# Second biases of an FFN and of eight experts taken off TensorE, zeros added into open sums, and the places of a tanh stage dealt out anew

## The chip, the cores and the metric

The kernel runs on one core of a Trainium2 chip. The metric is the device time of one execution in microseconds (us), and the figure compared is the median over runs.

## The reference, cut to what matters

The input is x, 4 batches of 1024 tokens, 256 wide, all in float32. The first layer is an additive cross-attention to 77 context rows of each batch; the second is a mixture of 8 experts beside a shared FFN.

```python
txt_proj = einsum('btd,de->bte', textual_features, Ws)
feat_proj = einsum('bfd,de->bfe', layernorm(x), W)
h = tanh(txt_proj[:, None, :, :] + feat_proj[:, :, None, :] + b)     # 1024 x 77 x 256 per batch
rho = einsum('bftd,d->bft', h, w[:, 0]) + (1 - qm)[:, None, :] * NEG
att = softmax(rho);  txt_h = einsum('bft,btd->bfd', att, textual_features)
x = x + tanh(txt_h @ Wcw.T + bcw) * layernorm(x) + tanh(txt_h @ Wcb.T + bcb)
...
y = layernorm(x)
probs = softmax(y @ gate)                                            # 4096 tokens, 8 experts
scores, token_idx = top_k(probs per expert, k=512)
out_tok = gelu(y[token_idx] @ W1 + b1) @ W2 + b2                      # 256 -> 1024 -> 256
routed = zeros.at[token_idx].add(out_tok * scores)
shared = gelu(y @ Ws1 + bs1) @ Ws2 + bs2
x = x + routed + shared
```

The two biases b2 and bs2 that are added after the second matrix product are the "second biases" of the title.

## The kernel before, in words

The kernel is one program with one list of steps, made by `work_order`. Every engine walks the whole list and runs the steps that are its own, in the list's order; semaphores carry the waits between engines. So an engine that waits at one step holds up all its later ones.

**The tanh stage** (0 to 602 us). Tokens are cut into 8 units of 512 (v = 0 to 7, two in a batch; `va` = 6 and `vb` = 7 are the last two). The 1024 x 77 x 256 tanh values of a batch are dealt into blocks of 128 x 4096, 157 in all (0 to 156). A block goes through three steps: `add` on VectorE (L1434: z = feat + one column of txt_bias, 8 adds of 128x512 where the block belongs to one unit, 4 of 128x1024 where it belongs to both units of a batch), `tanh` on ScalarE in place (L1042; a few "direct" pieces, L1038, have ScalarE do the add itself and VectorE none), and `rho` on TensorE (L828), which multiplies by w and adds into a bank of the unit that stays open until the unit's last block. There are 4 buffers z, so the adds of block n+4 need rho(n) to be over; from block 90 on rho goes two blocks at a time (`TOGETHER`). `SPLITS` tells which blocks are of both units, and so where a unit ends: unit 6 ends with block 144 and unit 7 with block 156.

Between the blocks stands everything else, at places given by the tables `PRE` (x's layer norm, its turn, the projection, of the next units), `TAIL` (what follows when a unit's sums are complete) and `FFN` (the shared FFN of units 0 to 5). What has place n comes behind add(n+2), tanh(n+1) and rho(n) in the list. The tail of a unit is, in order: rho_out and rho_turn; `att_shift` (VectorE, L1493 to L1497), `att_exp` (ScalarE, L1049), `weigh` (VectorE), `gate_in` (L1528, L1530), `gates` (ScalarE, L1053), `y_scale` (POOL, the nine small instructions from L1244 to L1257), `logits_shift` (VectorE, L1613 to L1617, reads POOL's y_ry), `y_norm` (POOL, L1173 and L1176), the turning of y on TensorE (L754), and four `whole` steps (POOL, L1300). These last complete the residual in x_ring.

The shared FFN runs m by m over 8 slices of 128 of H: `up` (TensorE L870, 6 matmuls), `gelu` (ScalarE, L1096), `down` (TensorE, L885, four 128x256 matmuls into two open banks). Before slice 0 the bias bs2 is put in by four matmuls (L881): a row of zeros and ones, `b2_row`, times `b2_s`, in which VectorE has split b2 and bs2 into two parts (`split_b2`, once, early). Then `down_end` (VectorE L1649) adds the banks to x_ring, and the result is stored.

**The router** (602 to 666 us). Unit 7's tail, the softmax of all logits and ten rounds of a threshold search, then ranks and lists. The FFN of units 6 and 7 is cut into 97 pieces which TensorE runs between the rounds ("filler").

**The experts** (666 to 862 us). For each expert `e_up` (L954), gelu, a split in two parts (`e_hi` ScalarE L1142, `e_lo` VectorE L1796), `e_down` and `e_sum` (L977). Before slice 0 four matmuls (L971) put in the bias b2; for the last expert there is one (L987) before each of its four tiles (L992). `e_out` (ScalarE L1150) scales a 128x256 tile by the tokens' scores, and POOL scatters it, adding, into the output (L1355). W1 and W2 of the next expert are loaded by SP and split meanwhile.

## Time and profile before

| | |
|---|---|
| median of 3 runs | 871.35 us (870.77 to 871.72) |
| the profiled execution, its device time | 871.33 us |
| its span, first to last instruction | 869.5 us |
| busy: TensorE, ScalarE, VectorE, POOL | 791.8, 752.7, 714.6, 272.1 us |
| mean granted TensorE clock | 0.983 of full speed |

Read it by stages: each engine's share over the whole span is a mean over three stages that have different limits. The time outside the span is 871.33 - 869.5 = 1.8 us.

### The profile page before, as it was taken

The numbers are of one execution on the slowest core, as the hardware profiler recorded it, in microseconds if no ns is written. First come the engines' busy times: TensorE is split into PE (matmuls) and PEld (weight loads), VectorE is DVE, ScalarE is ACT, GpSimd is POOL, SyncE is SP. The second block draws the span as 40 slices with busy tenths as digits, with TensorE's granted clock in tenths as the row PEclk, the third lists the DMA queues.
The fourth block names the chain that finished last, engine by engine and source line by source line (L and its number), as shares of the span: only waits on it lengthen the run. The fifth ranks groups of instructions, "written<-read, shape, count | busy, mean of one in ns | idle before, by whom it ended". The sixth has DMA issues, their size and how long they took to land.

```text
span 869.5 us, 13896 instructions
## 1 busy us (share of the span) xinstructions
PE 791.8 (91%) x5385; PEld 475.6 (55%) x5385; DVE 714.6 (82%) x1408; ACT 752.7 (87%) x556; POOL 272.1 (31%) x388
## 2 busy tenths in 40 slices
PE   7776677659999999999999999999999999999996
PEld 6321122214444344444444554564777999999986
DVE  4789999997979999999799989998887776666540
ACT  3999999999999999999999999988854676667672
POOL 3200430053505004784001360014504144555424
PEclk9798999999999999999999999999999999999999
DMA  7100000000001000200000010002203356554513
GB/s 258 33 1 1 1 1 1 1 25 25 2 1 49 1 1 1 98 1 2 25 1 1 25 49 1 25 2 76 95 25 106 126 133 147 146 144 100 135 21 41
DMA packets 32405, 41.81 MB, mean 48 GB/s; under 512 B 2365, under 2 KB 29011, under 8 KB 32339
## 3 DMA queue, kind: packets, MB, share of 16 engines
q1 hardware_dynamic: 26083, 32.49, 11.5%
q0 software_dynamic: 6144, 8.39, 5.7%
q8 instruction: 43, 0.70, 0.3%
q14 instruction: 23, 0.19, 0.1%
q10 hardware_dynamic: 112, 0.04, 0.0%
HBM read 28.33 MB, written 12.58 MB: 47 GB/s over the span
## 4 chain that ended last, share of the span: by engine, by line
PE 42%; ACT 40%; DVE 8%; issue 7%; POOL 2%; POOLq 0%; DVEq 0%; ACTq 0%
ACT z L1042 37%; PE bank L954 10%; PE bank L977 9%; PE bank L828 6%; PE bank L885 5%; DVE z L1434 5%; PE bank L870 4%; ACT u L1096 2%; PE bank L754 1%; PE bank L803 1%; PE bank L764 1%; PE bank L992 1%; POOL xn L1176 1%; PE bank L928 1%; PE bank L971 0%
## 5 line engine op out<-in xcount | busy, mean ns | idle before, releaser
L1042 ACT ACTIVATE z<-z 128x4096 f32<-128x4096 f32 (+3 forms) x157 | 536.1, 3481 | 5.9 <-DVE z L1434 5.9
L1434 DVE TENSOR_SCALAR z<-feat,txt_bias 128x1024 f32<-128x1024 f32 (+1 forms) x742 | 431.9, 655 | 18.9 <-PE bank L828 18.3
L828 PE MATMUL bank<-z,window 128*32 128x512 f32 x2464 | 298.4, 612 | 47.6 <-ACT z L1042 47.4
L828 PEld LDWEIGHTS bank<-z,window 128*32 128x32 f32 x2464 | 69.3, 111 | 230.8 <-issue 141.5
L885 PE MATMUL bank<-ws_sb,u 128*128 128x256 f32 x512 | 126.3, 388 | 0.7 <-ACT u L1096 0.6
L885 PEld LDWEIGHTS bank<-ws_sb,u 128*128 128x128 f32 x512 | 92.4, 190 | 35.2 <-issue 20.6
L870 PE MATMUL bank<-tr,ws_s 128*128 128x512 f32 x384 | 107.3, 417 | 2.3 <-ACT u L1096 1.6
L954 PE MATMUL bank<-xg_s,w_s 128*128 128x512 f32 x384 | 99.1, 396 | 0.2 <-DVE xg_s L1790 0.2
L1796 DVE TENSOR_TENSOR hid_s<-hid,hid_s 128x512 fp32r<-128x512 f32 x60 | 41.5, 692 | 59.2 <-ACT hid_s L1142 59.2
L977 PEld LDWEIGHTS bank<-w_s,hid_s 128*128 128x128 f32 x672 | 86.3, 188 | 3.9
L1244 POOL TENSOR_TENSOR scale<-wb,x_ry 128x4 f32<-128x4 f32 x7 | 3.8, 544 | 270.3 <-ACT wb L1053 270.3
L977 PE MATMUL bank<-w_s,hid_s 128*128 128x256 f32 x672 | 88.1, 280 | 0.0
L1132 ACT ACTIVATE hid<-bank,vec 128x512 f32<-128x512 f32 x64 | 44.1, 690 | 49.0 <-PE bank L954 48.9
L870 PEld LDWEIGHTS bank<-tr,ws_s 128*128 128x128 f32 x384 | 70.5, 188 | 29.2 <-issue 11.4
L954 PEld LDWEIGHTS bank<-xg_s,w_s 128*128 128x128 f32 x384 | 68.0, 188 | 12.1 <-DVE xg_s L1790 0.7
L1343 POOL DMA_INDIRECT xg<-xn_dram,idx x32 | 38.4, 1199 | 112.6 <-DVE idx L1779 105.3
L1355 POOL DMA_INDIRECT out_dram<-y,idx x32 | 57.5, 1798 | 30.8 <-ACT y L1150 22.9
L1096 ACT ACTIVATE u<-bank,vec 128x512 f32<-128x512 f32 x64 | 44.4, 704 | 10.7 <-PE bank L870 10.7
L1165 POOL TENSOR_SCALAR x_ve<-x_mv 128x4 f32<-128x4 f32 x7 | 4.3, 613 | 126.3 <-DVE x_less L1380 126.3
L1810 DVE TENSOR_TENSOR w_s<-w_raw,w_s 128x1024 fp32r<-128x1024 f32 (+1 forms) x36 | 39.2, 1103 | 1.3 <-ACT w_s L1117 1.3
L1142 ACT ACTIVATE hid_s<-hid 128x512 fp32r<-128x512 f32 x60 | 38.0, 633 | 1.9
L1176 POOL TENSOR_SCALAR xn<-x_ring,y_ry,offset 128x256 f32<-128x256 f32 x32 | 34.0, 1072 | 0.9
(263 smaller groups left out, 720.7 us busy)
## 6 DMA issues: line engine op xcount, KB each, us to landing
w_raw<-in_L_ffn_W_dram SPq DMA_DIRECT2D x16, 1024.0 KB, 5.6
x_ring<-in_x_dram SPq DMA_DIRECT2D x8, 512.0 KB, 7.9
xn_dram<-xn SPq DMA_DIRECT2D x8, 512.0 KB, 2.9
out_dram<-x_ring SPq DMA_DIRECT2D x8, 512.0 KB, 2.9
u<-in_L_ffn_Ws_dram SPq DMA_DIRECT2D x1, 1024.0 KB, 11.8
ws_sb<-in_L_ffn_Ws_dram SPq DMA_DIRECT2D x1, 1024.0 KB, 14.5
xg<-xn_dram,idx POOLq DMA_INDIRECT x32, 4.5
out_dram<-y,idx POOLq DMA_INDIRECT x32, 4.1
```

Source lines behind the costliest of these rows:

```text
L828: ins = e.matmul(sums[v][32 * g:32 * g + 32, :], window[:, c, 31 - at_row:63 - at_row], z[:, n % ZB, at_piece:at_piece + TOK], start=(v, g ...
L870: ins = e.matmul(dst[:], ws1_s[:, i, c, m * P:(m + 1) * P], tr[:, v % 2, j, c, :], start=n == 0, stop=n == passes - 1)
L885: ins = e.matmul(banks[DOWN[j // 2]][:, j % 2 * D:(j % 2 + 1) * D], u[:, m % UR, j * P:(j + 1) * P], ws2_sb[:, m, :], start=False, stop=m ...
L954: ins = e.matmul(dst[:], w1_s[k][:, i, c, m * P:(m + 1) * P], xg_s[:, k, j, c, :], start=c == 0 and n == 0, stop=c == C - 1 and n == 2)
L977: ins = e.matmul(part, parts[:, i, a * P:(a + 1) * P], w2_s[k][:, j, m, :], start=False, stop=(m == M - 1 and term == 2), skip_group_check ...
L1042: e.activation(part, part, ACT.Tanh).then_inc(signal(*step), 1)
L1096: e.activation(u[:, m % UR], banks[up_bank(v, m)][:], ACT.Gelu_apprx_tanh, bias=vec[:, col["bs1"] + m:col["bs1"] + m + 1]).then_inc(signal ...
L1132: e.activation(hid[:, m % HC, :], banks[UP[m % 2]][:], ACT.Gelu_apprx_tanh, bias=vec[:, cb:cb + 1]).then_inc(signal(*step), 1)
L1176: ins = e.tensor_scalar(dst[:, j, :], src[:, j, :], factor[:, j:j + 1], offset[:, j:j + 1], ALU.mult, ALU.add)
L1355: e.indirect_dma_start(out_rows, where, y[:, ex % 2, a, :], None, compute_op=ALU.add).then_inc(scattered, 16)
L1434: ins = e.tensor_scalar(z[:, n % ZB, i * width:(i + 1) * width], feat_of(units, c), bias_of(units, t, c), None, ALU.add)
L1796: e.tensor_tensor(parts[:, 1, :], hid[:, m % HC, :], parts[:, 0, :].bitcast(F32), ALU.subtract).then_inc(signal(*step), 1)
```

## The change

Seven things change together.

- The second biases leave TensorE. All 64 bias matmuls go: 32 L881, 28 L971 and 4 L987, and with them `split_b2`, one memset and four small DMAs.
- bs2 comes as `bs2_rep`, one row copied to all partitions, and a new POOL step `biased` adds it to x_ring behind the `whole` steps of each unit: four tensor_tensor 128x256, 32 in all. `down_end` now waits for it.
- b2 of all experts comes as `b2_rep` by a broadcast DMA of 1 MB (`load_b2`) behind the first expert's weights, into buffers that are dead by then. A new POOL step `bias_rows` multiplies it by the scores, four tensor_scalar 128x256 per expert at slice 3. `e_out` moves from ScalarE to VectorE: one instruction with bank, score and bias row.
- `stir`: 89 bf16 matmuls of zeros, 128x512, are added to the open sum: two behind rho of blocks 0 to 2 and 8 to 46, and one in the middle of a unit's logits where a sum is open. Three more matmuls on ident stand behind unit 0's logits.
- In the last batch 10 rows are shared by both units where there were 8: four blocks of one unit become blocks of both, unit 6 ends with block 146 and unit 7's own blocks are the last 10 rather than 12.
- Direct pieces in the first blocks are 28 where they were 24, and 1 later where there were 4.
- The tables PRE, TAIL and FFN, the number of filler pieces at each point of the router, and the place of unit 6's `down_end` are dealt out anew. The filler is 97 pieces in both.

```diff
-SPLITS = ((8, 20), (0, 20), (0, 20), (0, 8))
-FIRST_DIRECT = (6, 3, 0, 2, 2, 4, 0, 7)
+SPLITS = ((8, 20), (0, 20), (0, 20), (0, 10))
+FIRST_DIRECT = (7, 7, 1, 3, 1, 4, 0, 5)
 AHEAD = 3
-DIRECT = (8, 9, 126, 129)
+DIRECT = (12,)
...
-    (0, 0, 2, 2, 2, 2, 4, 4, 5, 10, 7, 7, 11, 11, 11),
+    (1, 1, 2, 1, 2, 2, 3, 4, 1, 5, 3, 7, 7, 8, 6),
...
-    (128, 130, 132, 133, 136, 136, 139, 142),
-    (143, 144, 145, 146, 147, 148, 149, 152),
+    (128, 129, 132, 133, 134, 137, 138, 140),
+    (143, 144, 145, 146, 148, 149, 149, 150),
...
-TOGETHER, TOGETHER_FROM = 2, 90
-BUSY = (20, 3, 5)
+TOGETHER, TOGETHER_FROM = 2, 92
+BUSY = (20, 3, 5, 3)
+STIRS = {n: 2 for n in (0, 1, 2, *range(8, 47))}
...
-END_PLACES = (3, 4)
-ENDS_BEHIND = 8
+END_PLACES = (10, 2)
+ENDS_BEHIND = 6
...
-FFN_PLACES = (-1, 1, 2)
+FFN_PLACES = (-1, 0, 2)
...
-                *[[("y_turned", v, c)] for c in range(C)], [("whole", v, j) for j in range(J)]]
+                *[[("y_turned", v, c)] for c in range(C)], [*(("whole", v, j) for j in range(J)), ("biased", v)]]
...
-              ("load_w1", 0), ("load_w2", 0), *end[2], ("att_exp", vb), ("early_probs",)]
+              ("load_w1", 0), ("load_w2", 0), ("load_b2",), *end[2], ("att_exp", vb), ("early_probs",)]
...
+        if m == 3:
+            steps.append(("bias_rows", ex))
...
-            for first in (0, B2_LOW):
-                e.dma_start(b2_raw[first:first + E, :], b2).then_inc(loaded["b2"], 16)
-                e.dma_start(b2_raw[first + E:first + E + 1, :], bs2.unsqueeze(0)).then_inc(loaded["b2"], 16)
+            e.dma_start(bs2_rep[:], bs2.partition_broadcast(P)).then_inc(loaded["bs2"], 16)
...
+                elif kind == "load_b2":
+                    e.wait_ge(*done("rho_turn", vb))
+                    e.dma_start(b2_rep[:], b2.rearrange("e d -> (e d)").partition_broadcast(P).rearrange("p (e d) -> p e d", e=E)
+                                ).then_inc(loaded["b2"], 16)
...
+            def stir(times):
+
+                if not stirred:
+                    e.wait_ge(consts, MASK_CLEAR)
+                    stirred.append(True)
+                held = [v for v in sums if all((v, g) in begun for g in range(G)) and any(left[v, g] for g in range(G))]
+                for _ in range(times if held else 0):
+                    e.matmul(sums[held[-1]][:], spare[:, 0:1].bitcast(BF16)[:, 0:1].broadcast_to([P, P]), ones_h[:], start=False,
+                             stop=False, skip_group_check=True)
...
+                    stir(STIRS.get(n, 0))
...
+                        if j == J // 2:
+                            stir(1)
...
-                        e.wait_ge(*done("split_b2"))
                     if m == 0:
-                        for j in range(first, end):
-                            dst = take(DOWN[j // 2]) if j % 2 == 0 else banks[DOWN[j // 2]]
-                            e.matmul(dst[:, j % 2 * D:(j % 2 + 1) * D], b2_row[:, E:E + 1].broadcast_to([B2_ROWS, P]), b2_s[:],
-                                     start=j % 2 == 0, stop=False, skip_group_check=True)
+                        for j in range(first + first % 2, end, 2):
+                            take(DOWN[j // 2])
                     e.wait_ge(*done("gelu", v, m))
                     for j in range(first, end):
                         ins = e.matmul(banks[DOWN[j // 2]][:, j % 2 * D:(j % 2 + 1) * D], u[:, m % UR, j * P:(j + 1) * P],
-                                       ws2_sb[:, m, :], start=False, stop=m == M - 1, skip_group_check=True)
+                                       ws2_sb[:, m, :], start=m == 0 and j % 2 == 0, stop=m == M - 1, skip_group_check=True)
...
-                        for a in range(A):
-                            e.matmul(sums_of[a // 2][:, a % 2 * D:(a % 2 + 1) * D], b2_row[:, ex:ex + 1].broadcast_to([B2_ROWS, P]), b2_s[:],
-                                     start=a % 2 == 0, stop=False, skip_group_check=True)
...
-                elif kind == "e_out":
-                    ex, a = args
-                    bank, left = (SUM[ex % 2][a // 2], a % 2 * D) if ex < E - 1 else (LAST_SUM[a], 0)
-                    e.wait_ge(*(done("e_sum", ex, a // 2) if ex < E - 1 else done("e_tile", a)))
-                    e.wait_ge(*done("scored", ex))
-                    if ex > 1:
-                        e.wait_ge(scattered, 16 * A * (ex - 1))
-                    e.activation(y[:, ex % 2, a, :], banks[bank][:, left:left + D], ACT.Identity,
-                                 scale=score[:, ex % NL, a:a + 1]).then_inc(signal(*step), 1)
...
+                elif kind == "biased":
+                    v, = args
+                    e.wait_ge(loaded["bs2"], 16)
+                    for j in range(J):
+                        row_of = x_ring[:, v % XB, j, :]
+                        e.wait_ge(*done("whole", v, j))
+                        ins = e.tensor_tensor(row_of, row_of, bs2_rep[:], ALU.add)
+                    ins.then_inc(signal(*step), 1)
...
+                elif kind == "bias_rows":
+
+                    ex, = args
+                    e.wait_ge(loaded["b2"], 16)
+                    e.wait_ge(*done("scored", ex))
+                    if ex > 1:
+                        e.wait_ge(*done("e_out", ex - 2, A - 1))
+                    for a in range(A):
+                        ins = e.tensor_scalar(bias_rows[:, ex % 2, a, :], b2_rep[:, ex, :], score[:, ex % NL, a:a + 1], None, ALU.mult)
                     ins.then_inc(signal(*step), 1)
...
-                    e.wait_ge(*done("whole", v, J - 1))
+                    e.wait_ge(*done("biased", v))
...
+                elif kind == "e_out":
+                    ex, a = args
+                    bank, left = (SUM[ex % 2][a // 2], a % 2 * D) if ex < E - 1 else (LAST_SUM[a], 0)
+                    e.wait_ge(*done("bias_rows", ex))
+                    e.wait_ge(*(done("e_sum", ex, a // 2) if ex < E - 1 else done("e_tile", a)))
+                    e.wait_ge(*done("scored", ex))
+                    if ex > 1:
+                        e.wait_ge(scattered, 16 * A * (ex - 1))
+                    e.scalar_tensor_tensor(out=y[:, ex % 2, a, :], in0=banks[bank][:, left:left + D],
+                                           scalar=score[:, ex % NL, a:a + 1], in1=bias_rows[:, ex % 2, a, :], op0=ALU.mult,
+                                           op1=ALU.add).then_inc(signal(*step), 1)
...
-                elif kind == "split_b2":
-                    low = slice(B2_LOW, 2 * B2_LOW)
-                    e.wait_ge(loaded["b2"], 64)
-                    e.tensor_tensor(b2_row[:], ident[0:B2_ROWS, 0:E + 1], ident[0:B2_ROWS, B2_LOW:B2_LOW + E + 1], ALU.add)
-                    link(e.tensor_copy(b2_s[:], b2_raw))
-                    e.wait_ge(vector_link, linked)
-                    e.tensor_tensor(b2_s[low, :], b2_raw[low, :], b2_s[low, :].bitcast(F32),
                                     ALU.subtract).then_inc(signal(*step), 1)
```

The rows below are each engine's instructions in program order. First TensorE at the first expert, before (`xg` are the gathered tokens, L954 is e_up, L971 the bias, L977 e_down):

```order
L754 MATMUL bank<-ident,xg 128x128 x8
L954 MATMUL bank<-xg_s,w_s_126 128x512 x18
L971 MATMUL bank<-b_s,b_row 128x256 x4
L977 MATMUL bank<-w_s_127,hid_s 128x256 x12
L954 MATMUL bank<-xg_s,w_s_126 128x512 x6
```

and after, where L772 is the turn of xg, L972 is e_up and L990 is e_down:

```order
L772 MATMUL bank<-ident,xg 128x128 x8
L972 MATMUL bank<-xg_s,w_s_125 128x512 x18
L990 MATMUL bank<-w_s_126,hid_s 128x256 x12
L972 MATMUL bank<-xg_s,w_s_125 128x512 x6
L990 MATMUL bank<-w_s_126,hid_s 128x256 x12
```

The bias rows are gone and nothing stands in their place on TensorE.

Next the tail of unit 6, which falls on the last dozen blocks of the tanh stage. VectorE before, at `att_shift` (L1434 are the adds, eight to a block, and two at the end of unit 6 or 7; L1486 is rho_out, L1649 down_end, L1493 to L1497 att_shift):

```order
L1486 COPY rho_sb<-bank 128x512
L1649 TENSOR_TENSOR x_ring<-bank,x_ring 128x512 x2
L1434 TENSOR_SCALAR z<-feat,txt_bias 128x512 x16
L1493 TENSOR_REDUCE bank<-bank 128x4
L1495 TENSOR_REDUCE sm<-bank 128x4
L1497 TENSOR_TENSOR att<-bank,sm 128x320
```

and after, where L1455 are the adds, L1507 is rho_out and L1514 and L1516 begin att_shift:

```order
L1455 TENSOR_SCALAR z<-feat,txt_bias 128x512 x34
L1507 COPY rho_sb<-bank 128x512
L1455 TENSOR_SCALAR z<-feat,txt_bias 128x512 x8
L1514 TENSOR_REDUCE bank<-bank 128x4
L1516 TENSOR_REDUCE sm<-bank 128x4
L1518 TENSOR_TENSOR att<-bank,sm 128x320
```

The adds of four blocks now stand ahead of rho_out, and those of one more between rho_out and att_shift. Before, two blocks' adds stood there. VectorE again, from the last step of `weigh` to `logits_shift` (L1613 to L1617) of unit 6, before:

```order
L1521 TENSOR_REDUCE wb<-att_tmp 128x8
L1434 TENSOR_SCALAR z<-feat,txt_bias 128x512 x16
L1528 TENSOR_TENSOR wb<-wb,sm 128x8
L1530 TENSOR_TENSOR wb<-wb,bc 128x8
L1434 TENSOR_SCALAR z<-feat,txt_bias 128x512 x34
L1613 TENSOR_TENSOR lg<-lg,y_ry 128x32
L1615 TENSOR_REDUCE sm<-lg 128x4
```

and after (L1634 to L1638 are logits_shift, which occurs for two units in a row here):

```order
L1542 TENSOR_REDUCE wb<-att_tmp 128x8
L1455 TENSOR_SCALAR z<-feat,txt_bias 128x512 x8
L1549 TENSOR_TENSOR wb<-wb,sm 128x8
L1551 TENSOR_TENSOR wb<-wb,bc 128x8
L1455 TENSOR_SCALAR z<-feat,txt_bias 128x512 x8
L1634 TENSOR_TENSOR lg<-lg,y_ry 128x32
L1636 TENSOR_REDUCE sm<-lg 128x4
L1638 TENSOR_TENSOR lg<-lg,sm 128x32
L1455 TENSOR_SCALAR z<-feat,txt_bias 128x512 x8
L1634 TENSOR_TENSOR lg<-lg,y_ry 128x32
L1636 TENSOR_REDUCE sm<-lg 128x4
L1638 TENSOR_TENSOR lg<-lg,sm 128x32
```

Before, 34 adds, those of four blocks, stand between gate_in (L1530) and logits_shift; now 16 adds, two blocks, stand between gate_in (L1551) and unit 6's logits_shift, the second of the two, and one block's adds follow it. ScalarE at the same tail, before (L1042 tanh, L1096 gelu, L1049 att_exp, L1053 gates):

```order
L1042 ACTIVATE z<-z 128x4096
L1049 ACTIVATE att<-att 128x320
L1096 ACTIVATE u<-bank,vec 128x512
L1042 ACTIVATE z<-z 128x4096
L1096 ACTIVATE u<-bank,vec 128x512
L1042 ACTIVATE z<-z 128x4096
L1053 ACTIVATE wb<-wb 128x8
```

and after, with L1055 for tanh, L1109 for gelu, L1062 for att_exp and L1066 for gates:

```order
L1055 ACTIVATE z<-z 128x4096 x2
L1062 ACTIVATE att<-att 128x320
L1109 ACTIVATE u<-bank,vec 128x512
L1055 ACTIVATE z<-z 128x4096
L1109 ACTIVATE u<-bank,vec 128x512 x2
L1055 ACTIVATE z<-z 128x4096
L1109 ACTIVATE u<-bank,vec 128x512
L1055 ACTIVATE z<-z 128x4096
L1066 ACTIVATE wb<-wb 128x8
```

The exp now stands one tanh later (behind tanh 149 rather than 148), and gates behind tanh 152 rather than 150.

Last POOL in the middle of the tanh stage, around `y_norm` of unit 3, before:

```order
L1169 TENSOR_TENSOR y_ry<-y_ve,minus_half 128x4
L1257 TENSOR_TENSOR y_ry<-y_ry,scale 128x4
L1173 TENSOR_TENSOR offset<-x_less,y_ry 128x4
L1176 TENSOR_SCALAR xn_113<-x_ring,y_ry,offset 128x256 x4
L1244 TENSOR_TENSOR scale<-wb,x_ry 128x4
```

and after (L1303 is whole, L1311 biased, L1177 and L1180 y_norm):

```order
L1173 TENSOR_TENSOR y_ry<-y_ve,minus_half 128x4
L1260 TENSOR_TENSOR y_ry<-y_ry,scale 128x4
L1303 TENSOR_SCALAR x_ring<-x_ring,scale,shift 128x256 x4
L1311 TENSOR_TENSOR x_ring<-x_ring,bs_rep 128x256 x4
L1177 TENSOR_TENSOR offset<-x_less,y_ry 128x4
L1180 TENSOR_SCALAR xn_112<-x_ring,y_ry,offset 128x256 x4
L1303 TENSOR_SCALAR x_ring<-x_ring,scale,shift 128x256 x4
```

Before, y_norm followed the y_scale chain at once, and no `whole` stood between them. Now `whole` and `biased` of unit 2 stand between the chain and y_norm of unit 3.

## Rows read from the trace of the kernel before

**Rows 1.** The page: span, busy times, and TensorE's granted clock in 40 slices.
```profile
span 869.5 us, 13896 instructions
...
PE 791.8 (91%) x5385; PEld 475.6 (55%) x5385; DVE 714.6 (82%) x1408; ACT 752.7 (87%) x556; POOL 272.1 (31%) x388
...
PEclk9798999999999999999999999999999999999999
```

**Rows 2.** Windows: start:end length, busy by engine (x instructions), clock, DMA.
```profile
180.00:454.00 274.00, 256.54 (x1708) 118.36 (x1704) 250.28 (x421) 273.74 (x106) 90.28 (x102) 0.99 0.06 18
454.00:606.00 152.00, 150.03 (x970) 82.25 (x970) 140.81 (x295) 146.44 (x72) 37.63 (x54) 1.00 0.06 22
606.00:666.00 60.00, 59.15 (x343) 46.55 (x344) 48.38 (x188) 36.05 (x94) 17.57 (x25) 1.00 0.20 63
666.00:862.00 196.00, 195.30 (x1448) 177.69 (x1446) 120.03 (x184) 131.75 (x204) 88.89 (x59) 1.00 0.48 117
340.00:400.00 60.00, 58.64 (x392) 29.57 (x391) 58.51 (x105) 59.77 (x26) 49.89 (x53) 1.00 0.11 36
```

**Rows 3.** The waits of the span: us in total, times, longest.
```profile
ACT z L1042 <- DVE z L1434: 5.9, 5, 3.8
```

**Rows 4.** Timeline of TensorE: start, length, what, [idle before it <-releaser].
```profile
696.51 0.63 PE L971 MATMUL bank<-b_s,b_row 128*128 128x256 f32 x4
696.97 1.57 PE L977 MATMUL bank<-w_s,hid_s 128*128 128x256 f32 x12
...
852.53 0.28 PE L987 MATMUL bank<-b_s,b_row 128*128 128x256 f32 x1
852.65 1.59 PE L992 MATMUL bank<-w_s,hid_s 128*128 128x256 f32 x12
```

**Rows 5.** Groups of instructions by line: count, busy us, mean ns, idle before.
```profile
L1150 ACT ACTIVATE y<-bank,score 128x256 f32<-128x256 f32 x32 | 12.7, 470 | 9.1 <-PE bank L992 7.5 <-DMA out_dram<-y,idx 1.6
L1723 DVE SCALAR_TENSOR_TENSOR scan<-scan,off,gt 128x256 f32<-128x256 f32 x1 | 0.5, 484 | 0.1
L1317 POOL TENSOR_TENSOR scan<-probs,vals 128x256 f32<-128x256 f32 x1 | 0.8, 769 | 0.1
L1176 POOL TENSOR_SCALAR xn<-x_ring,y_ry,offset 128x256 f32<-128x256 f32 x32 | 34.0, 1072 | 0.9
```

**Rows 6.** Timeline of ScalarE at unit 6's tail.
```profile
570.54 3.71 ACT L1042 ACTIVATE z<-z 128x4096 f32<-128x4096 f32 x1
...
578.58 3.63 ACT L1042 ACTIVATE z<-z 128x4096 f32<-128x4096 f32 x1 [3.75 <-DVE z L1434]
582.11 0.19 ACT L1053 ACTIVATE wb<-wb 128x8 f32<-128x8 f32 x1
...
597.95 4.56 ACT L1042 ACTIVATE z<-z 128x4096 f32<-128x4096 f32 x2
```

**Rows 7.** Timeline of VectorE at unit 6's tail.
```profile
568.68 0.49 DVE L1497 TENSOR_TENSOR att<-bank,sm 128x320 f32<-128x320 f32 x1
...
575.30 6.42 DVE L1434 TENSOR_SCALAR z<-feat,txt_bias 128x512 f32<-128x512 f32 x16
...
589.28 7.71 DVE L1434 TENSOR_SCALAR z<-feat,txt_bias 128x512 f32<-128x512 f32 x16 [0.80 <-PE bank L828]
```

**Rows 8.** Timeline of TensorE: rho in unit 6's tail and at the stage's end.
```profile
570.08 3.64 PE L828 MATMUL bank<-z,window 128*32 128x512 f32 x32
...
600.86 4.50 PE L828 MATMUL bank<-z,window 128*32 128x512 f32 x36
```

**Rows 9.** Timeline of POOL at unit 6's tail.
```profile
582.38 0.22 POOL L1244 TENSOR_TENSOR scale<-wb,x_ry 128x4 f32<-128x4 f32 x1 [59.77 <-ACT wb L1053]
...
588.60 0.20 POOL L1257 TENSOR_TENSOR y_ry<-y_ry,scale 128x4 f32<-128x4 f32 x1
...
592.66 3.66 POOL L1300 TENSOR_SCALAR x_ring<-x_ring,scale,shift 128x256 f32<-128x256 f32 x4
```

**Rows 10.** Timeline of POOL and TensorE around unit 3's y_norm and its turn.
```profile
359.44 5.03 POOL L1176 TENSOR_SCALAR xn<-x_ring,y_ry,offset 128x256 f32<-128x256 f32 x4
...
377.85 1.04 PE L754 MATMUL bank<-ident,xn 128*128 128x128 f32 x8
```

50 lines of the change are left out of this document (24 added, 26 removed), and 34 rows, old and new, of tables (FFN, PRE, TAIL).

## The prediction

> **What bounds the kernel now.** I read the page first, then busy time by stage, the chain of waits, and at last the timelines of the places where the order changes. The page [rows 1] shows three engines busy for more than 80% of the span and none for all of it, so the shares of the whole span say little and the stages must be read apart [rows 2].
>
> In the tanh stage the bound is ScalarE: from 180 to 454 us it is busy 273.74 of 274 us, while VectorE has 250.28 and TensorE 256.54. Towards its end, 454 to 606 us, that is no longer clean: ScalarE has 146.44 of 152, TensorE 150.03. Part of the missing time is one wait. The list of waits [rows 3] has ScalarE five times, 5.9 us in total, behind VectorE's adds, and the longest, 3.8, is found in the timeline before the tanh at 578.58 [rows 6]: VectorE was in unit 6's tail, whose att_shift ended at 569.17, and began the next adds only at 575.30 [rows 7]. The other four waits, 5.9 - 3.8 = 2.1 us, lie in the first 70 us or are as short.
>
> In the router TensorE is busy 59.15 of 60 us, and in the experts 195.30 of 196, at a full clock in both. There every microsecond taken off TensorE should come off the span, as long as what replaces it finds room: ScalarE has 131.75 of 196, VectorE 120.03, POOL 88.89 [rows 2].
>
> The sum is made against the profiled run, 871.33 us, which is 0.02 below the median of 871.35, so the two may be taken as one. I call 0.2% (1.7 us) about what a measurement of this kernel can tell from no change.
>
> **The experts: -3.7 us.** The four bias matmuls of an expert start at 696.51, and the next matmul at 696.97: 0.46 us [rows 4]. There are seven such groups, 3.2 us. In the last expert one costs 852.65 - 852.53 = 0.12 us, four of them 0.5. Together 3.7. What comes instead: e_out leaves ScalarE (0.470 us a piece) and becomes one VectorE instruction; the nearest one, of the same kind with 256 columns, takes 0.484 [rows 5]. VectorE has 76 us of room in this stage, so 32 x 0.48 = 15.5 us hide there; without cover an e_out late by 0.5 us would delay a bank that is needed only two experts later. bias_rows costs POOL four operations of 0.77 (a plain one on two inputs) to 1.07 us (one with a scalar per row) [rows 5], 3.1 to 4.3 us of about 24.5 per expert, beside 11.1 busy. It stands at slice 3 of its own expert, and the scatter that needs its result comes later, so it hides. The last e_outs are 0.01 us longer. The 1 MB broadcast falls where the DMA engines are busy 20% [rows 2]; it delays nothing but, at the worst, the second expert's weights.
>
> **The router: -0.7 us.** The biases of units 6 and 7 were eight matmuls among the filler, at 0.12 us 0.9 us. TensorE has 0.85 us of idle time in the stage, and the rounds of the search are a chain, so I take 0.7; the bounds are 0 and 0.9. The new deal of 97 filler pieces changes no amount of work.
>
> **The tanh stage: -1.1 us, the least certain term.** It has three parts.
>
> Early, -0.5. The split of b2 leaves VectorE, its waits in the first stretch can shrink by up to 2.1 us, and four more direct pieces move work from VectorE to ScalarE, which costs that engine some. TensorE's clock is at a mean of 0.7 to 0.8 in two of the first four slices [rows 1], the lower of its levels for part of them. The zeros may raise it there, but ScalarE is the bound and TensorE's speed reaches it only through a freed buffer. The bounds are +0.5 and -2.1; I take -0.5.
>
> Unit 6's tail, +0.6. Today's wait of 3.75 us comes because att_shift, weigh and all between stand in one stretch on VectorE, with no adds among them, until 575.30. Now the adds of five blocks stand ahead of att_shift, ScalarE has its work for that stretch, and this wait goes. But two others can take its place.
> (a) att_exp now stands behind tanh 149 and waits for att_shift, which stands behind the adds of block 151. These need the buffer that rho(147) frees. At the places of today rho(146) and rho(147) run from 570.08 to 573.72 [rows 8], while tanh 149 ends at 570.54 + 3.71 = 574.25 [rows 6]. Adds of 3.21 us (6.42 for two blocks, [rows 7]) and about 1.2 us of att_shift end at 573.72 + 4.4 = 578.1, 3.9 us after the tanh; and up to 4.4 if rho_out is late as well. The other end is 0, if TensorE runs four microseconds less behind. It has one bias group less here and the FFN of units 4 and 5 ends two blocks sooner. I take 2.
> (b) gates now stand behind tanh 152. POOL's y_scale runs from 582.38 to 588.80, 6.4 us [rows 9], then comes logits_shift (0.6) and then the adds of block 155 (3.2): 10.2 us, against two tanhs of 3.5 net, 7.0. The wait is 3.2 us. The other end is 0, if POOL's chain is shorter or the adds run ahead. I take 2.4, nearer the upper end, as only the place isn't measured.
> Together 4.4 against 3.75: +0.6, bounds -3.7 and +3.9.
>
> The end, -1.2. After the last tanh, 602.51 [rows 6], TensorE still works until 600.86 + 4.50 = 605.36 [rows 8], so 2.85 us of the stage are its lag. FFN work of unit 5 now ends at place 150 rather than 152, and the waits above let TensorE catch up. What must follow the last tanh is at least the rho of the last small block, 4 of the 36 matmuls: 4.50 - 3.64 = 0.86 us [rows 8]; with the block before it, 3.64 / 2 = 1.82, it is 2.7. I take 1.65, near the middle: a gain of 1.2, bounds 0 and 2.
>
> biased adds 32 operations of 0.77 to 1.07 us to POOL, 3.1 to 4.3 us a unit. POOL has 274 - 90 us free in the middle of the stage, and down_end comes blocks later: 0. Without that cover two banks of TensorE would stay taken for up to 4.3 us a unit. Four blocks as two-unit blocks cost VectorE 4 adds of 1024 instead of 8 of 512: less work, no cost.
>
> **The sum**: 3.7 + 0.7 + 1.1 = 5.5 us, 871.3 - 5.5 = **865.8 us**.
>
> **Rivals.**
> (R1) More comes off: TensorE is nearly full from 454 to 606 us too, so bias groups of 0.46 us there count as well, and one of the two stalls doesn't come. That gives a further 2 to 4 us, 861.8 to 864. For it: 150.03 of 152; against: the order of steps says that both waits exist. 0.22.
> (R2) The tail takes more: stalls (a) and (b) at their upper bounds, 7.6 us against 3.75, and no gain at the end: +3.9 instead of -0.6, less 0.5 early: total -1.7 to -3.7, 867.6 to 869.6. For it: the 10 us by which rho trails tanh there. 0.17.
> (R3) POOL slows VectorE. Two blocks' adds take 6.42 us when POOL is idle, but 7.71 at 589.28 while POOL works from 588.60 to 596.32 [rows 7, 9]: 1.29 us in 7.7, or 0.17 us lost per us of POOL. The 32 new operations are 25 to 34 us, so VectorE loses 4.2 to 5.8 us. If all of it reached the path the change would stand at -1.3 to +0.3, some 870.8 us. Against: VectorE has 24 us of room from 180 to 454. 0.08 for within 0.2%.
> The Trainium skill says in "GPSIMD Engine Reference", Key points, that GpSimd shares its SBUF interfaces with VectorE and contends with instructions that have two SBUF inputs or use a 2-port mode. The trace agrees that the adds stretch; the rule would put the time at R3's 870.8, the rows on room at the forecast.
> (R4) Slower. Between POOL's y_scale and y_norm of unit 3 there now stand whole and biased of unit 2, 3.66 [rows 9] plus 3.1 to 4.3 us. y_norm is then 7 to 8 us late. If its turn on TensorE stands early in the new order, TensorE waits with rho queued behind it, no buffer comes free, and ScalarE waits 8 us: 871.3 - 5.5 + 8 = 873.8. It decides once the wait is over 5.5 + 1.7 = 7.2 us. For it: POOL is busy 49.89 of 60 us from 340 to 400 us, and ScalarE has nothing to spare [rows 2]. Against: y_norm now runs 359.44 to 364.47 and the next turn of such rows is at 377.85 [rows 10], 13.4 us of slack. 0.08.
>
> **How the numbers follow.** The forecast, 864 to 867.6 us, has 0.45, R1 0.22, R2 0.17, R3 0.08, R4 0.08. The time is the forecast's, 865.8. The range 862.2 to 869.6 takes in all of the forecast and R2 and most of R1, some 0.8; it leaves out R3, R4 and R1's far end. Faster by over 0.2% are the forecast, R1 and R2, 0.84; within 0.2% R3, 0.08; slower R4, 0.08.
>
> **What would show it.** Right: no bias groups on TensorE; the experts' stretch 3.7 us shorter with TensorE still full; one wait of ScalarE before att_exp (about 2) and one before tanh 155 or so (about 2.4) in place of the one of 3.75; rho ending 1.5 to 2 us after the last tanh; the router shorter by 0.7. Wrong: new idle time of TensorE in the experts behind e_out (banks) or gathered rows; a wait of TensorE on xn (L754's successor) near 370 us; ScalarE waiting for adds between 180 and 454 us; the tail's waits above 7 us. The forecast falls most easily on the tail, where both stalls are reckoned from an order and from durations of a schedule that will not be the same.

## The result, and the profile after

The changed kernel takes 870.65 us (median of 21 runs, 867.72 to 871.6) where the kernel before takes 871.77 (21 runs, 870.4 to 872.84). The ratio is 0.9985, with an interval of 0.9978 to 0.9991. So the change gains 1.1 us of the 5.5 that were forecast, and the time lies above the forecast's range of 862.2 to 869.6. It is faster, but by less than the 0.2% that I called telling.

The page of the changed kernel, the same lines as [rows 1]:

```profile
span 869.4 us, 14023 instructions
...
PE 802.7 (92%) x5397; PEld 473.0 (54%) x5416; DVE 735.8 (85%) x1420; ACT 741.0 (85%) x525; POOL 328.4 (38%) x451
...
PEclk9899999999999999999999999999999999999999
```

The profiled execution took 871.19 us, against 871.33 before; both are near their medians. VectorE has 21 us more work and POOL 56. The stages, start:end and length, busy by engine, granted clock and DMA, as in [rows 2]:

```profile
180.00:454.00 274.00, 255.08 (x1698) 117.15 (x1696) 255.59 (x422) 272.84 (x106) 106.01 (x125) 0.99 0.06 18
454.00:606.00 152.00, 148.48 (x955) 79.25 (x953) 141.20 (x280) 145.37 (x70) 44.31 (x66) 1.00 0.07 22
606.00:666.00 60.00, 55.95 (x305) 44.19 (x305) 49.85 (x187) 35.93 (x94) 20.23 (x29) 0.97 0.22 76
666.00:862.00 196.00, 194.96 (x1443) 176.68 (x1443) 135.30 (x218) 120.08 (x172) 127.34 (x92) 1.00 0.48 119
```

The third line is the new thing: in the router TensorE was busy 59.15 us at a full clock, now 55.95 at 0.97. Three points of the timeline give the account. The end of the tanh stage, at the turn of the last unit's sums on TensorE, was 606.15 and is 606.18. The first turn of gathered rows, where the experts begin, was 665.93 and is 669.48: 3.5 us later. The last matmul ended at 861.6 and ends at 861.35. So the tanh stage gave 0.0 (forecast -1.1), the router took +3.5 (forecast -0.7), and the experts gave -3.8 (forecast -3.7). The first of these is the least sure: two traces of one and the same tanh stage, those of the kernel before and of run 3 below, differ by 0.85 us at that point (606.15 and 605.30).

The router's loss sits at one instruction. Timeline of VectorE in the changed kernel, in the threshold search (start, length, instruction):

```profile
624.69 0.09 DVE L1700 DVE_READ_ACCUMULATOR reached<-bank 128x1 f32 x1
624.81 2.63 DVE L1708 SCALAR_TENSOR_TENSOR candidate<-steps_of,digit,offered 128x7 f32<-128x7 f32 x1
627.48 0.48 DVE L1690 TENSOR_SCALAR_CACHE_REDUCE gt<-hid,candidate 128x256 f32<-128x256 f32 x1
```

POOL at the same time:

```profile
624.64 2.78 POOL L1311 TENSOR_TENSOR x_ring<-x_ring,bs_rep 128x256 f32<-128x256 f32 x4
```

And the same VectorE instruction in the kernel before, when POOL was through:

```profile
624.95 0.23 DVE L1688 SCALAR_TENSOR_TENSOR candidate<-steps_of,digit,offered 128x7 f32<-128x7 f32 x1
```

Seven columns that took 0.23 us take 2.63, and end at 627.44, when POOL's four additions of `biased` for unit 7 end (627.42). The search is a chain through this instruction, and TensorE has no filler left for the round. Its timeline and the windows right behind it:

```profile
629.23 0.18 PE L921 MATMUL bank<-cnt,same_expert_h 128*128 128x7 bf16 x1 [2.12 <-DVE hid L1690]
```

```profile
624.00:628.00 4.00, 2.73 (x14) 2.06 (x13) 3.71 (x7) 0.77 (x5) 3.42 (x6) 1.00 0.00 0
628.00:632.00 4.00, 2.77 (x11) 2.29 (x12) 3.40 (x19) 3.72 (x13) 0.00 (x0) 0.84 0.02 4
632.00:636.00 4.00, 4.00 (x16) 3.19 (x15) 2.57 (x12) 1.66 (x7) 0.00 (x0) 0.73 0.01 2
```

After standing idle TensorE is granted 0.84 and 0.73 of its clock for eight microseconds (part of them at the lower level, 1.2 GHz), where it had 1.00 before. The filler runs slower and the rounds' counts queue behind it: the next decisions come 2.1, 3.0 and 4.0 us later than before. In runs 2, 8 and 9 below, in which nothing holds that instruction for longer than 0.64 us, the clock is 1.00 in all these windows.

In the tanh stage gains and losses cancel. Tanh 46 ends at 186.4 rather than 189.0 and tanh 90 at 351.0 rather than 353.2; by tanh 149 nothing is left (574.3 in both). ScalarE's waits in between, and the two in unit 6's tail, in the changed kernel:

```profile
378.44 3.62 ACT L1055 ACTIVATE z<-z 128x4096 f32<-128x4096 f32 x1 [0.50 <-DVE z L1455]
382.69 3.62 ACT L1055 ACTIVATE z<-z 128x4096 f32<-128x4096 f32 x1 [0.62 <-DVE z L1455]
545.37 3.62 ACT L1055 ACTIVATE z<-z 128x4096 f32<-128x4096 f32 x1 [0.62 <-DVE z L1455]
549.86 7.14 ACT L1055 ACTIVATE z<-z 128x4096 f32<-128x4096 f32 x2 [0.87 <-DVE z L1455]
...
576.18 0.47 ACT L1062 ACTIVATE att<-att 128x320 f32<-128x320 f32 x1 [1.88 <-DVE att L1518]
...
598.53 4.57 ACT L1055 ACTIVATE z<-z 128x4096 f32<-128x4096 f32 x2 [1.94 <-DVE z L1455]
```

The last two are the waits (a) and (b) of the prediction, 1.88 and 1.94 us where I took 2 and 2.4. The first four, 2.6 us, I did not foresee.

### The profile page after: what moved, and what is told of

Its sections match the earlier page's. It is cut to its first block, busy times and chain, and to the rows that moved or that the text cites. A ratio compares the mean times of both kernels' runs of the same rounds, so it can differ in the third digit from the quotient of the medians.

```text
span 869.4 us, 14023 instructions
## 1 busy us (share of the span) xinstructions
PE 802.7 (92%) x5397; PEld 473.0 (54%) x5416; DVE 735.8 (85%) x1420; ACT 741.0 (85%) x525; POOL 328.4 (38%) x451
## 4 chain that ended last, share of the span: by engine, by line
ACT 47%; PE 34%; DVE 8%; issue 7%; POOL 2%; POOLq 0%; ACTq 0%; DVEq 0%
ACT z L1055 42%; PE bank L972 10%; PE bank L990 9%; DVE z L1455 5%; PE bank L903 5%; PE bank L846 3%; PE bank L891 3%; ACT u L1109 2%; ACT z L1051 2%; PE bank L782 1%; PE bank L772 1%; PE bank L1005 1%; PE bank L946 1%; POOL out_dram L1376 1%; ACT hid L1094 0%
## 5 line engine op out<-in xcount | busy, mean ns | idle before, releaser
L1055 ACT ACTIVATE z<-z 128x4096 f32<-128x4096 f32 (+5 forms) x157 | 535.6, 3481 | 4.6 <-DVE z L1455 4.6
L1455 DVE TENSOR_SCALAR z<-feat,txt_bias 128x1024 f32<-128x1024 f32 (+1 forms) x725 | 437.5, 677 | 23.3 <-PE bank L846 22.7
L846 PEld LDWEIGHTS bank<-z,window 128*32 128x32 f32 x2464 | 67.3, 110 | 213.8 <-issue 131.3
L903 PEld LDWEIGHTS bank<-ws_sb,u 128*128 128x128 f32 x512 | 94.8, 192 | 37.2 <-issue 23.7
L972 PE MATMUL bank<-xg_s,w_s 128*128 128x512 f32 x384 | 99.1, 396 | 0.2 <-DVE xg_s L1810 0.2
L990 PEld LDWEIGHTS bank<-w_s,hid_s 128*128 128x128 f32 x672 | 86.7, 188 | 4.5
L990 PE MATMUL bank<-w_s,hid_s 128*128 128x256 f32 x672 | 88.1, 280 | 0.0
L972 PEld LDWEIGHTS bank<-xg_s,w_s 128*128 128x128 f32 x384 | 68.0, 188 | 12.1 <-DVE xg_s L1810 0.7
L1109 ACT ACTIVATE u<-bank,vec 128x512 f32<-128x512 f32 x64 | 43.6, 692 | 10.5 <-PE bank L891 10.4
L1349 POOL TENSOR_SCALAR bias_rows<-b_rep,score 128x256 f32<-128x256 f32 x32 | 40.4, 1778 | 0.0
```

The lines of the kernel that those rows point to most:

```text
L846: ins = e.matmul(sums[v][32 * g:32 * g + 32, :], window[:, c, 31 - at_row:63 - at_row], z[:, n % ZB, at_piece:at_piece + TOK], start=(v, g ...
L903: ins = e.matmul(banks[DOWN[j // 2]][:, j % 2 * D:(j % 2 + 1) * D], u[:, m % UR, j * P:(j + 1) * P], ws2_sb[:, m, :], start=m == 0 and j % ...
L972: ins = e.matmul(dst[:], w1_s[k][:, i, c, m * P:(m + 1) * P], xg_s[:, k, j, c, :], start=c == 0 and n == 0, stop=c == C - 1 and n == 2)
L990: ins = e.matmul(part, parts[:, i, a * P:(a + 1) * P], w2_s[k][:, j, m, :], start=m == 0 and a % 2 == 0 and term == 0, stop=(m == M - 1 an ...
L1055: e.activation(part, part, ACT.Tanh).then_inc(signal(*step), 1)
L1109: e.activation(u[:, m % UR], banks[up_bank(v, m)][:], ACT.Gelu_apprx_tanh, bias=vec[:, col["bs1"] + m:col["bs1"] + m + 1]).then_inc(signal ...
```

## The experiments

Theory A: a VectorE instruction on two tensors that meets POOL's group of two-tensor additions is kept out until the group ends. Theory B: the new deal of filler starves TensorE. Theory C: the same additions stretch VectorE's adds in the tanh stage and ScalarE comes to wait. Theory D: they stand in POOL's queue ahead of work that others need.

The kernel before took 871.77 us beside runs 1 to 4, 871.48 beside runs 5 to 8 and 872.11 beside runs 9 to 12, and each ratio is to the one beside it. Runs from different groups are therefore best compared by their ratios. The profiles by stage: where TensorE begins to turn the last unit's sums (the end of the tanh stage), from there to the first turn of gathered rows (the router), and from there to the last matmul (the experts), in us:

| | tanh stage ends | router | experts |
|---|---|---|---|
| before | 606.15 | 59.8 | 195.7 |
| changed | 606.18 | 63.3 | 191.9 |
| run 1 | 606.4 | 60.8 | 192.3 |
| run 2 | 606.7 | 59.4 | 191.9 |
| run 3 | 605.3 | 59.8 | 195.7 |
| run 4 | 609.5 | 62.8 | 191.9 |
| run 5 | 604.7 | 60.7 | 192.3 |
| run 6 | 607.1 | 63.3 | 191.9 |
| run 7 | 605.2 | 59.8 | 195.7 |
| run 8 | 604.9 | 59.8 | 191.8 |
| run 9 | 606.7 | 60.1 | 191.9 |
| run 10 | 608.2 | 65.9 | 191.9 |
| run 11 | 604.0 | 59.8 | 191.8 |
| run 12 | 605.6 | 59.8 | 191.9 |

**1. Unit 7's biased behind the first gather.**

```diff
-    order += [("y_shift_last", vb), *end[13]]
+    order += [("y_shift_last", vb), *(step for step in end[13] if step[0] != "biased")]
...
-    order += [*high, ("fold", 0), ("folded", 0), ("gather", 0), ("scored", 0)]
+    order += [*high, ("fold", 0), ("folded", 0), ("gather", 0), ("scored", 0), ("biased", vb)]
```

> Theory A (POOL holds VectorE): in the changed kernel one small VectorE instruction of the threshold search lasts 2.63 us, from 624.81 to 627.44, and the four adds of biased for unit 7 run on POOL from 624.64 to 627.42. The two are tied: VectorE cannot get at its operands while POOL works through the group, TensorE then runs dry and its granted clock falls. Here biased for unit 7 stands behind the first gather on POOL, after the search, and nothing else is changed. Expected by A: the 2.63 becomes 0.23, the clock in the search stays at full, the first expert comes 3.5 us sooner, and the time is 870.65 - 3.5 = 867.2 us (866.5 to 868). Theory B (the new deal of filler pieces starves TensorE in the search, and the long instruction is a chance of the profile): 870.6 us, the clock dip stays.

Measured 869.39 us (7 runs, 868.18 to 870.47; ratio to the kernel before 0.9973, 0.9962 to 0.9984). That is 1.3 us off the changed kernel, not 3.5, and outside the expected 866.5 to 868. The search is whole again, its instruction takes 0.23. But the group now meets another VectorE instruction on two tensors. VectorE and POOL in this run:

```profile
660.38 5.50 DVE L1780 TENSOR_TENSOR onehot<-slot_c,iota_slot_h 128x512 bf16<-128x512 int32 x4
```

```profile
662.55 2.77 POOL L1311 TENSOR_TENSOR x_ring<-x_ring,bs_rep 128x256 f32<-128x256 f32 x4
```

Four such instructions at 0.69 would take some 2.7 us; here it is 5.5, and the excess is again POOL's 2.8. All of it falls on the last of the four, which lasts 3.64 us from 662.23. By the trace it had begun 0.3 us before POOL's group, so an instruction that is already running can be held too. The theory holds and the remedy was bad: the hold had moved.

**2. Unit 7's biased reads one tensor.** A multiplication by 1.0 in the addition's place; unit 7 lacks bs2.

```diff
-                        ins = e.tensor_tensor(row_of, row_of, bs2_rep[:], ALU.add)
+                        if v == vb:
+                            ins = e.tensor_scalar(row_of, row_of, 1.0, None, ALU.mult)
+                        else:
+                            ins = e.tensor_tensor(row_of, row_of, bs2_rep[:], ALU.add)
```

> The four operations of biased for unit 7 stay where they are on POOL but read one tensor rather than two (a multiplication by 1.0; the bias bs2 is left out for unit 7). Theory A in its narrow form (only a POOL operation on two tensor inputs keeps VectorE's instruction out): 867.2 us, and the small VectorE instruction takes 0.2 to 0.5 us. Theory A in its wide form (any POOL work there keeps it out): 870.6 and an instruction of over 2 us. Theory B: 870.6 with no tie to the instruction.

Measured 868.33 us (867.25 to 869.29; ratio 0.996, 0.9947 to 0.9973): 2.3 less than the changed kernel. Its profiled run took 867.83 us, 3.4 less than that of the changed kernel, and no VectorE instruction of the search is long. The one that falls into POOL's group (625.16 to 628.46):

```profile
625.33 0.25 DVE L1711 SCALAR_TENSOR_TENSOR candidate<-steps_of,digit,offered 128x7 f32<-128x7 f32 x1
```

It began 0.17 us after the group's start, as in the changed kernel, and took 0.25. POOL works on the same rows at the same place, only with one tensor (0.84 to 0.86 us each, so the group is even longer), and so it is the second tensor that keeps VectorE out. The router is 59.4 us long here, 0.4 less than before: that is what the eight bias matmuls were worth. The medians differ by less than the profiles because the changed kernel's profiled run lies 0.5 us above its median and this one's 0.5 below. Three of the changed kernel's 21 runs took 867.7 to 868.3 us, as long as this run. They may be runs in which the two instructions missed each other; that is not shown, as no trace has such a run.

**3. The additions alone, in the kernel before**, for unit 7 only, with rows of Ws2 as the added tensor.

```diff
+                    for j in range(J):
+                        row_of = x_ring[:, v % XB, j, :]
+                        e.wait_ge(*done("whole", v, j))
+                        ins = e.tensor_tensor(row_of, row_of, ws2_sb[:, j, :].bitcast(F32), ALU.add)
```

> The kernel before, with one thing added: behind the whole steps of unit 7 POOL adds rows of another tensor to x_ring, four tensor_tensor 128x256 as biased does (so unit 7's output has a wrong addend). There the small VectorE instruction starts at 624.95 and POOL's group would run from about 624.6 to 627.4. Theory A: that instruction takes 2.4 us more, the clock falls behind it, and the time is 871.8 + 2.4 to 4 = 874.2 to 875.8 us. Theory B (the deal is the cause, which this kernel does not have): 871.8 us.

Measured 871.82 us (11 runs, 870.42 to 873.08; ratio 1.0): nothing. A miss for theory A as I had put it. VectorE and POOL:

```profile
624.10 0.35 DVE L1696 SCALAR_TENSOR_TENSOR candidate<-steps_of,digit,offered 128x7 f32<-128x7 f32 x1
```

```profile
623.70 2.80 POOL L1308 TENSOR_TENSOR x_ring<-x_ring,ws_sb 128x256 f32<-128x256 f32 x4
```

The instruction fell into the group, 0.40 us after its start, and was over at 624.45, when the first of the four additions ended, after only 0.35. In the changed kernel it began 0.17 us after the group's start and was kept out through all four. So a meeting does not always mean a hold over the whole group. What decides it stays open: the start within the group is one difference, the added tensor another. The added tensor is not all of it: in run 4, with bs2 added, a VectorE instruction of 128x32 on two tensors met the third of unit 6's four additions (601.95 to 602.86), took 0.72 us for 0.18 and was over at 602.91, before the fourth ended at 603.55. A second small instruction of run 3 met the last addition and took 0.43 for 0.16.

**4. The code alone.** The new code with all old tables and without zeros.

```diff
-STIRS = {n: 2 for n in (0, 1, 2, *range(8, 47))}
+STIRS = {}
...
-FFN_PLACES = (-1, 0, 2)
+FFN_PLACES = (-1, 1, 2)
```

> The code of the change (second biases on POOL and VectorE) with the places, splits, direct pieces and fills of the kernel before, and without the added zero matmuls. Theory A: the experts give 3.6 us, the router 0.7 for its eight bias matmuls, and the held instruction takes 3.5 back: 871.8 - 4.3 + 3.5 = 871.0 us (870 to 871.5), with one VectorE instruction of over 2 us in the search. Theory B: the old deal does not starve TensorE, so 871.8 - 4.3 = 867.5 us.

Measured 872.31 us (12 runs, 870.3 to 874.56; ratio 1.001, 1.0 to 1.002). Its search has the long instruction too (2.65 us), with the old fill: theory B is out (in run 7 the new fill alone leaves the router at 59.8 us, as before). But the sum is 1.3 above what A alone gave, and the profiled run (874.0) is 2.7 above the kernel before though its experts take 3.7 us less. The last tanh ends at 606.4 us rather than 602.5. The waits of ScalarE on adds are 9.3 us (nine times) instead of 5.9, and VectorE's adds are longer while POOL adds. VectorE, then POOL:

```profile
382.88 7.77 DVE L1453 TENSOR_SCALAR z<-feat,txt_bias 128x1024 f32<-128x1024 f32 x8
```

```profile
384.02 4.59 POOL L1309 TENSOR_TENSOR x_ring<-x_ring,bs_rep 128x256 f32<-128x256 f32 x4
```

**5. The code alone, biased on one tensor in all units.** bs2 is left out.

```diff
-                        ins = e.tensor_tensor(row_of, row_of, bs2_rep[:], ALU.add)
+                        ins = e.tensor_scalar(row_of, row_of, 1.0, None, ALU.mult)
```

> The code of the change with the old places and without zero matmuls, as in the run of the code alone (872.3 us, tanh stage ending at 606.4 where it was 602.5), but all 32 operations of biased read one tensor and not two (the bias bs2 is left out). Their number, their place on POOL and the waits on them stay. Theory C (POOL's adds on two tensors stretch VectorE's adds, 1.08 us where they take 0.75, and ScalarE comes to wait for them): the tanh stage ends at 602.5 to 603.5, no instruction of the search is held, and the time is 871.8 - 4.3 = 867.5 us (866.5 to 868). Theory D (biased and whole stand in POOL's queue ahead of work that others wait for): the tanh stage still ends near 606 and the time is 869.5 to 871.

Measured 866.45 us (865.24 to 867.83; ratio 0.9942, 0.9929 to 0.9954), 5.9 us less than run 4, at the lower end of the expected 866.5 to 868. The last tanh ends at 601.5. The same eight adds, with POOL at the substitute (383.38 to 389.31):

```profile
382.12 6.49 DVE L1453 TENSOR_SCALAR z<-feat,txt_bias 128x1024 f32<-128x1024 f32 x8
```

```profile
383.38 5.93 POOL L1309 TENSOR_SCALAR x_ring<-x_ring 128x256 f32<-128x256 f32 x4
```

There is an add every 0.97 us in run 4 (7.77 / 8) and every 0.81 here (6.49 / 8). The adds that lie wholly beside POOL's group took 1.21 to 1.23 us in run 4 and 0.87 to 0.88 here; with POOL idle one takes 0.75. POOL's queue is as long as before (the group even takes 5.93 us rather than 4.59), so with the old places theory D is out and C stands. ScalarE's waits on adds fall from 9.3 to 4.9 us (three).

**6. The changed kernel without zeros.**

```diff
-STIRS = {n: 2 for n in (0, 1, 2, *range(8, 47))}
+STIRS = {}
...
-                        if j == J // 2:
-                            stir(1)
...
-    order += [("logits", 0), ("busy", 3)]
+    order += [("logits", 0)]
```

> The changed kernel without the 89 zero matmuls and the three extra ones behind unit 0's logits. In it tanh 46 ends at 186.4 us where the kernel before has 189.0, and the code alone, without zeros and with the old places, 188.7. Theory S (the zeros raise TensorE's granted clock early, buffers come free sooner): tanh 46 ends at 188.5 or later, and of the 2.3 us at least 1 stays to the end: 871.6 to 872.9 us. Theory T (the new places and the four more direct pieces made that gain): tanh 46 still ends near 186.5 and the time is 870.6 us.

Measured 870.93 us (12 runs, 868.13 to 872.03; ratio 0.9991, 0.9983 to 1.0). The zeros are worth 0.3 us, or 0.5 by the ratios, no more than the scatter. Tanh 46 ends at 186.9 rather than 186.4. The granted clock from 0 to 30 us is 0.84 without and 0.89 with them, and 0.94 and 0.96 from 90 to 180; it hardly reaches ScalarE. Theory S is out. The held instruction is there as well (2.62 us).

**7. The deal alone.** The kernel before with the new tables.

> The kernel before with the new tables alone (splits, direct pieces, places, fills), second biases on TensorE as before and no zeros. Theory F (the deal is good by itself): from the code alone to the whole change the tanh stage got 3.3 us shorter, some 2.3 of it early; what is not the zeros' is the deal's, 1 us: 870.8 us. Theory G (the deal fits only the program without bias matmuls and costs elsewhere): 872 us or more.

Measured 869.76 us (11 runs, 869.06 to 870.62; ratio 0.9985, 0.9976 to 0.9993). So the new tables alone give what the whole change gives, and theory G is out. Tanh 46 ends at 187.5, tanh 90 at 352.1 and the last tanh at 602.1.

**8. The FFN's bias back on TensorE.** The changed kernel with the L881 matmuls and `split_b2` of before, and no biased.

```diff
-                        for j in range(first + first % 2, end, 2):
-                            take(DOWN[j // 2])
+                        for j in range(first, end):
+                            dst = take(DOWN[j // 2]) if j % 2 == 0 else banks[DOWN[j // 2]]
+                            e.matmul(dst[:, j % 2 * D:(j % 2 + 1) * D], b2_row[:, E:E + 1].broadcast_to([B2_ROWS, P]), b2_s[:],
+                                     start=j % 2 == 0, stop=False, skip_group_check=True)
```

> The changed kernel with the shared FFN's bias bs2 put back on TensorE: 32 matmuls and their set-up return, biased goes from POOL; the experts' bias stays off TensorE, deal and zeros stay. If POOL's two-tensor adds were what ate the gain (theories A and C), the experts' 3.6 and the early 2.3 us remain and the router pays its eight bias matmuls, 0.7: 871.8 - 3.6 - 2.3 + 0.3 = 866.2 us (865.5 to 867.5). If the bias matmuls in the tanh stage cost as much as POOL's adds did (TensorE 98% busy from 454 to 606 us), 868.5 to 870.

Measured 866.32 us (866.05 to 867.05; ratio 0.9943, 0.9931 to 0.9956). It computes all of the reference and is 4.3 us faster than the changed kernel, or 3.7 by the ratios. The four waits between 378 and 550 us are down to one of 0.23, and the search has no long instruction. In the profiles 1.3 us of the gain lie in the tanh stage and 3.5 in the router. The 32 bias matmuls cost less than the 32 additions that replaced them.

**9. whole and biased of unit 7 alternate on POOL.**

```diff
+                    if v == vb and j < J - 1:
+                        e.wait_ge(loaded["bs2"], 16)
+                        e.wait_ge(*done("whole", v, j))
+                        e.tensor_tensor(row_of, row_of, bs2_rep[:], ALU.add)
```

> The changed kernel, but for unit 7 the four whole (one tensor read, 0.55 us each) and the four additions of biased (two tensors, 0.72 each) alternate on POOL; the amount of work is the same. Theory A1 (a VectorE instruction on two tensors that meets POOL's group is kept out until the group of two-tensor operations ends, and gets in at the first other operation): the held instruction lasts 0.3 to 1.2 us, not 2.6, and the time is 870.65 - 2 to 3 = 867.6 to 868.6 us. Theory A2 (it is kept out by any unbroken POOL work of which part is on two tensors): still over 2 us, 870.6.

Measured 868.66 us (868.3 to 869.34; ratio 0.9964, 0.9952 to 0.9977), 2.0 less than the changed kernel (1.8 by the ratios) with the same work. The instruction meets two of the additions, each with a `whole` or nothing behind it, and each holds it until that addition ends (625.91 and 628.76):

```profile
625.35 0.58 DVE L1712 SCALAR_TENSOR_TENSOR candidate<-steps_of,digit,offered 128x7 f32<-128x7 f32 x1
...
628.14 0.64 DVE L1712 SCALAR_TENSOR_TENSOR candidate<-steps_of,digit,offered 128x7 f32<-128x7 f32 x1
```

**10. The group doubled.** bs2 is added twice to unit 7.

```diff
+                    if v == vb:
+                        for j in range(J):
+                            e.wait_ge(pool_link, linked - J + 1 + j)
+                            ins = e.tensor_tensor(x_ring[:, v % XB, j, :], x_ring[:, v % XB, j, :], bs2_rep[:], ALU.add)
```

> The changed kernel with the additions of biased for unit 7 made twice, eight in a row on POOL (bs2 is added twice to unit 7's rows). A1: the held instruction lasts as long as the group, 2.63 + 4 x 0.68 = 5.4 us, and the time rises by at least the 2.7 us: 873.4 to 875. If the length of the hold is not the group's (a fixed one of 2.6 us, from another cause): 870.6.

Measured 875.59 us (874.3 to 876.18; ratio 1.0037, 1.0023 to 1.0051). VectorE and POOL:

```profile
626.89 5.36 DVE L1714 SCALAR_TENSOR_TENSOR candidate<-steps_of,digit,offered 128x7 f32<-128x7 f32 x1
```

```profile
626.73 2.78 POOL L1311 TENSOR_TENSOR x_ring<-x_ring,bs_rep 128x256 f32<-128x256 f32 x4
629.47 2.76 POOL L1317 TENSOR_TENSOR x_ring<-x_ring,bs_rep 128x256 f32<-128x256 f32 x4
```

5.36 us for seven columns, as 5.4 was expected: the hold is as long as the group. With 9 and 10 the tie is shown by dose in both directions. The whole time is 0.6 us above the expected range. In the profile the router is 2.6 us longer than the changed kernel's, as expected; another 2.0 lie in the tanh stage, with a new wait of 1.17 us before tanh 42, and nothing in the edit explains them.

**11 and 12. The two waits of unit 6's tail**, on the kernel of run 8. The first moves logits_shift one place later in the list, the second also att_shift one earlier. Both are edits to the last row of `TAIL`; the upper pair of lines is run 11, the lower run 12.

```diff
-    (1, 1, 2, 1, 2, 2, 3, 4, 1, 5, 3, 7, 7, 8, 6),
+    (1, 1, 2, 1, 2, 2, 3, 4, 1, 6, 3, 7, 7, 8, 6),
...
-    (1, 1, 2, 1, 2, 2, 3, 4, 1, 6, 3, 7, 7, 8, 6),
+    (1, 1, 1, 1, 2, 2, 3, 4, 1, 6, 3, 7, 7, 8, 6),
```

> The changed kernel with the FFN's bias on TensorE (866.3 us), and unit 6's logits_shift one place later, behind the adds of block 155 rather than 154. Its trace has ScalarE waiting 1.92 us before tanh 155. The prediction's step (b) puts that down to VectorE waiting in logits_shift for POOL's y_scale ahead of the adds of 155. If so, the wait goes and the tanh stage ends 1.9 us sooner, of which TensorE's lag gives back up to 0.8: 864.4 to 865.2 us. If the wait is for a buffer (rho(151)), it stays: 866.3.

Measured 865.44 us (864.85 to 865.79; ratio 0.9925, 0.9911 to 0.9938), the best of all and 0.2 above the expected range. The wait of 1.9 before tanh 155 is gone and the last tanh ends at 599.7 rather than 601.8, but the last rho ends at 603.2 rather than 603.7: TensorE's lag behind ScalarE has grown from 1.9 to 3.5 us and takes back 1.6 of the 2.1 us, twice what was allowed for it.

> As the run before it, and unit 6's att_shift one place earlier too, behind the adds of block 150 rather than 151. ScalarE waits 2.06 us in att_exp behind tanh 149. By the prediction's step (a) the adds of 151 stand ahead of att_shift and cost 3.2 us there: the wait shrinks to 0 to 0.5 and another 1 to 1.9 us come off, 863 to 864.2 us. If att_shift really waits for TensorE's rho_turn, the wait stays near 2 and the time that of the run before.

Measured 866.98 us (866.7 to 867.27; ratio 0.9943, 0.9929 to 0.9957), 1.5 worse. ScalarE in this run, then VectorE at att_shift:

```profile
574.64 0.47 ACT L1072 ACTIVATE att<-att 128x320 f32<-128x320 f32 x1 [2.06 <-DVE att L1521]
586.06 3.63 ACT L1065 ACTIVATE z<-z 128x4096 f32<-128x4096 f32 x1 [1.61 <-DVE z L1458]
```

```profile
573.38 0.17 DVE L1517 TENSOR_REDUCE bank<-bank 128x4 f32<-128x8 f32 x1 [3.65 <-PE bank L870]
```

The wait in att_exp stays at 2.06, so it was not for the adds of 151. L870 is rho_turn: VectorE now stands idle for 3.65 us until TensorE has turned unit 6's sums, with those adds behind it, and they come late: 1.61 new.

## Why the prediction was wrong, point by point

**The experts, -3.7: right.** -3.8 measured. e_out on VectorE takes 0.476 us (0.484 was taken). bias_rows kept POOL busy for 40.4 us, 1.26 a piece against 0.77 to 1.07, a mis-sized term that the free time there covered for seven experts. For the last one it did not quite: VectorE stands idle for 3.4 us until the last bias row is ready at 855.44, and behind the late e_out the four scatters follow each other without a pause. The last one starts 1.0 us after the last matmul ends (861.35) where it was 0.8, so 0.2 of the 3.8 are lost again.

**The router, -0.7: the step that failed.** The prediction prices all 32 additions of biased at 0, from POOL's free time and from down_end coming later, and its sum for the router doesn't name unit 7's four at all. It looked only at POOL's queue and at the reader of the result. What they cost lies on another engine that has no dependence on them: VectorE's two-tensor instruction is held 2.4 us, TensorE runs dry behind it, its clock falls, and the router comes to +3.5 in the profiled run. Runs 2, 9 and 10 show the hold. The gain that was forecast is there beneath it, but smaller: 0.4 in run 2.

**"biased ... down_end comes blocks later: 0": the same error in the tanh stage.** R3 had the mechanism, but I priced it at 0.17 us per us of POOL work, from POOL's operations on one tensor, and gave it 0.08 since VectorE had 24 us of room. Runs 4 and 5 put it at 4 to 5 us on the path with the old places (the last tanh ends at 606.4 and 601.5, the waits on adds differ by 4.4); with the new places the four new waits are 2.6, and the last tanh ends 1.0 to 1.3 us later than in runs 7 and 8, which have no biased. The mean room of a long window was no cover: the adds are late at single places where there are two or three blocks ahead at the most. The result is nearest to R3, at 870.65 against its 870.8, but that is luck: R3 knew one of the two mechanisms and put all of the loss on VectorE's adds, while the larger part lies in the search. The page's rule that I cited beside R3 (the Trainium skill, "GPSIMD Engine Reference", Key points) names contention with VectorE instructions that have two SBUF inputs. The traces agree for the held instruction of the search, which has two; they add that the hold can last as long as POOL's group (5.36 us), and that POOL's multiplications, on one tensor, did not hold it (0.25 us in run 2).

**Early, -0.5: mis-sized.** -2.3 to -2.7 up to tanh 90, beyond even the bound of -2.1. The new places and direct pieces alone give 1.2 to 1.6 of it (run 7). The zeros give 0.5 at the most (run 6), and the rest is left for the split of b2 and the scatter: tanh 46 ends between 186.2 and 187.9 in traces of the changed kernel and of runs 1, 2, 9 and 10, whose programs are alike up to there.

**Unit 6's tail, +0.6: near in size (+0.1), wrong in one cause.** (a) 1.88 and (b) 1.94 for 2 and 2.4, together 3.8 against 3.75 before. (b) is as described (run 11). (a) is not the adds of 151 but rho_turn, which TensorE reaches late (run 12). That (a) came out at nearly the size forecast is luck. **The end, -1.2: it came to -1.0** between the last tanh and the last rho (2.85 us became 1.9), but the last tanh was 0.6 later.

**R2's sum is wrong.** With both stalls at their upper bounds and no gain at the end it is -3.7 - 0.7 - 0.5 + 3.9 = -1.0, or 870.3 us, and not 867.6 to 869.6. So the range that was made to hold all of R2 left out R2's own far end. The mechanism was another all the same: the two stalls came at 3.8 us and not at 7.6.

**R4 came in small.** TensorE waits for y_norm's rows near 370 us in the changed kernel:

```profile
374.57 1.09 PE L772 MATMUL bank<-ident,xn 128*128 128x128 f32 x8 [1.60 <-POOL xn L1180]
```

That is 1.6 us and not 8, and ScalarE's two waits of 0.50 and 0.62 follow it. Without biased (runs 7 and 8) TensorE doesn't wait there and neither does ScalarE. With the new places no run separates this from theory C; with the old ones run 5 says C. R1's tail gain did not come either.

## What to carry to other kernels

Work that is moved to an idle engine is hidden only if it shares nothing with the busy one: before calling POOL's work free, look which VectorE instructions run beside it, and how many tensors each of the two reads. A group of such POOL operations is best broken up with others, or put where no chain passes through VectorE. And a small total can hide large terms: of this change the tables gave 1.3 us (run 7, by the ratio) and the experts' bias 3.8, and the FFN's bias, moved for the same reason, took 3.7 to 4.3 of it back (run 8).

## What the runs showed of the hardware

A VectorE instruction of 128x7 on two tensors took 0.23 us alone. When it met POOL's tensor_tensor additions of 128x256 it took 0.58 and 0.64 with a single one (run 9), 2.62 to 2.65 with four in a row (the changed kernel, runs 4 and 6) and 5.36 with eight (run 10). Beside four multiplications by a scalar on POOL it was not held (0.25, run 2); beside POOL's conversions of 128x256 to bf16, earlier in the search, it took 0.40 to 0.72, so work on one tensor isn't always free either. One meeting with four additions cost only 0.35 (run 3), and I can't say why. VectorE's tensor_scalar adds, with one tensor, were never held but stretched: one of 128x1024 took 0.75 us alone, 1.21 to 1.23 beside POOL's additions and 0.87 to 0.88 beside its multiplications. It goes both ways: POOL's `whole` on 128x256 took 0.55 to 0.57 us in the router and 1.48 to 1.49 beside VectorE's adds at 363 to 367 us.
